# A four-layer graph network on one core: the first turning of x read from memory, row inverses on VectorE, the negated adjacency on ScalarE, and a new order of all parts

## What is computed

```python
# x (64,128,384), adj (64,128,128)
# L0: 12 heads: softmax over edges of (q k^T / sqrt(32) + beta*adj, masked where adj is 0), times v
# L1, two times: u = masked sums of (h Wl^T) h^T and (h Wr^T) h^T;  e = exp(u) * adj
#     attention = e / (sum(e) + 1e-10);  h = relu(layer_norm(attention @ h_lin))
# L2, two times (the digraph layer):
u = einsum('bid,bjd->bij', h, h) / temper
a = softmax(u, axis=-1)
delta = a * adjacency_matrix
attn = delta / (sum(delta, axis=-1) + 1e-10)
ctx = (attn*upper) @ hl + diag(attn) * hs + (attn*lower) @ hr
h = relu((ctx - mean) / sqrt(var + 1e-12) * g + beta)
# L3: 12 heads: softmax(q k^T * 384**-0.5 + adj) @ v, then @ Wo.T + bo
x = layernorm(x + L0(x, adj)); x = layernorm(x + L1(x, adj)); x = layernorm(x + L2(x, adj)); x = layernorm(x + L3(x, adj))
```

## Time and profile before

| what | value |
|---|---|
| median of 3 runs | 2648.01 us (2646.37 to 2648.55) |
| the profiled execution: its time | 2648.33 us |
| the profiled execution: its span, first to last instruction | 2646.3 us |
| PE busy | 2513.5 us, 95% |
| POOL, DVE, ACT busy | 2230.9, 2112.3, 2075.7 us |
| mean granted TensorE clock | 0.984 of 2.4 GHz |

### The profile page before, as it was taken

One profiled execution on the slowest core, in us unless ns is written; L12 is line 12 of the kernel. 1 busy time (PEld: TensorE's weight loads), 2 busy tenths in 40 slices (PEclk: granted clock), 3 DMA queues, 4 the chain that ended last, 5 costly groups with the idle time before them and its releaser, 6 DMA issues.

```text
span 2646.3 us, 91774 instructions
## 1 busy us (share of the span) xinstructions
PE 2513.5 (95%) x33856; PEld 1892.1 (71%) x33856; DVE 2112.3 (80%) x8230; ACT 2075.7 (78%) x5844; POOL 2230.9 (84%) x3340
## 2 busy tenths in 40 slices
PE   5799999999999999999999999999999999999985
PEld 4667677777777777777777777777777777777753
DVE  6687787877778888888888888888888888888874
ACT  6667877778778888888888788788788888888765
POOL 5488888888888898898888888888888888888874
PEclk9899999999999999999999999999999999999997
DMA  6834545545445555545545555554545555554533
GB/s 176 176 68 83 97 85 97 96 83 97 89 87 97 95 90 97 97 89 95 97 89 100 93 90 98 96 91 93 96 95 92 93 99 88 96 97 88 94 55 71
DMA packets 846822, 251.63 MB, mean 95 GB/s; under 512 B 805552, under 2 KB 845616, under 8 KB 846384
## 3 DMA queue, kind: packets, MB, share of 16 engines
q1 hardware_dynamic: 837920, 230.83, 50.3%
q10 hardware_dynamic: 8464, 14.94, 1.9%
HBM read 35.92 MB, written 12.58 MB: 18 GB/s over the span
## 4 chain that ended last, share of the span: by engine, by line
POOL 35%; PE 23%; DVE 16%; ACT 13%; issue 7%; DMA 5%; SPq 1%; DVEq 0%; ACTq 0%; POOLq 0%
POOL region L750 6%; ACT region L870 5%; DMA region<-region 4%; POOL region L739 4%; DVE region L1138 4%; PE bank L966 3%; PE bank L957 3%; PE bank L968 3%; PE bank L967 3%; PE bank L959 3%; PE bank L958 3%; ACT region L876 3%; POOL ab L766 3%; POOL region L790 2%; DVE small L1144 2%
## 5 line engine op out<-in xcount | busy, mean ns | idle before, releaser
L957 PE MATMUL bank<-region,w_hi 128*128 128x128 f16 x3960 | 690.4, 220 | 35.6 <-DVE w_lo L1075 14.0
L959 PE MATMUL bank<-region,w_lo 128*128 128x128 f16 x3960 | 690.0, 220 | 0.0
L958 PE MATMUL bank<-region,w_hi 128*128 128x128 f16 x3960 | 690.0, 220 | 0.0
L966 PE MATMUL bank<-w_hi,region 128*128 128x384 f16 x1815 | 595.5, 328 | 10.4 <-DMA region<-region 9.2
L967 PE MATMUL bank<-w_lo,region 128*128 128x384 f16 x1815 | 594.3, 327 | 0.0
L968 PE MATMUL bank<-w_hi,region 128*128 128x384 f16 x1815 | 594.2, 327 | 0.0
L750 POOL TENSOR_TENSOR region<-region 128x512 f16<-128x512 f32 x330 | 382.9, 1161 | 117.7 <-ACT region L876 116.6
L870 ACT ACTIVATE region<-region,small 128x128 f32<-128x128 f32 x1320 | 419.2, 389 | 53.6 <-DVE small L1144 44.1
L957 PEld LDWEIGHTS bank<-region,w_hi 128*128 128x128 f16 x3960 | 389.4, 98 | 60.8 <-issue 36.2
L958 PEld LDWEIGHTS bank<-region,w_hi 128*128 128x128 f16 x3960 | 389.8, 98 | 14.8 <-issue 9.9
L959 PEld LDWEIGHTS bank<-region,w_lo 128*128 128x128 f16 x3960 | 389.9, 98 | 0.0
(11 more groups left out here) (246 smaller groups left out, 8238.0 us busy)
## 6 DMA issues: line engine op xcount, KB each, us to landing
region<-region SPq DMA_TRANSPOSE x825, 3.0
last_unit<-w_dram ACTq DMA_DIRECT2D x19, 576.0 KB, 6.2
x<-x_dram SPq DMA_DIRECT2D x55, 192.0 KB, 2.3
out_dram<-region SPq DMA_DIRECT2D x55, 192.0 KB, 2.2
adj<-adj_dram SPq DMA_DIRECT2D x55, 64.0 KB, 2.2
mask<-adj_t_dram SPq DMA_DIRECT2D x55, 64.0 KB, 2.4
rows<-rows_dram ACTq DMA_DIRECT2D x5, 576.0 KB, 4.4
last_unit<-last_unit SPq DMA_TRANSPOSE x135, 3.1
```

Of the source, the lines that this page charges most:

```text
L957: pe.matmul(dst, lhsT=w_hi[:, w, k, cols], rhs=t_hi[u][:, k, :], start=(k == 0), stop=False)
L958: pe.matmul(dst, lhsT=w_hi[:, w, k, cols], rhs=t_lo[u][:, k, :], start=False, stop=False)
L959: last = pe.matmul(dst, lhsT=w_lo[:, w, k, cols], rhs=t_hi[u][:, k, :], start=False, stop=(k == DT - 1))
L966: pe.matmul(dst, lhsT=t_hi[u][:, k, :], rhs=w_hi[:, w, k, :], start=(k == 0), stop=False)
```

## The change

1. The host also passes x turned (`x_t_dram`). A new SP part `load_turned` loads it into the unit's `z` buffer, after norm 3 of unit i-7. ACT casts from there straight into the place that the transpose filled, and POOL writes the low half beside it. `turn` 0 on SP is gone, and projections 0 to 2 wait for POOL instead of a landing. The plain load of x and adj is a part of its own now, behind ACT's first cast; `bias_x` 0 on POOL and `masks` on DVE wait for it.
2. `denominator` is gone from POOL; its two steps follow on DVE behind the row sum, the inverse with `reciprocal`.
3. `minus_adjacency` goes from POOL to ACT.
4. The waits for weights go by the place of a weight in each engine's queue.
5. `PERIOD`, `SHIFTED` and nearly all wanted times in `PARTS` are new. Of the table two rows stand here for the rest.

```diff
-PERIOD = 22.1046
+PERIOD = 22.0572
-    (POOL, "sums", 0): (-457.777, 0.870, 0.950, ((VECTOR, "delta_di", 0),), ()),
+    (VECTOR, "delta_di", 0): (-124.527, 0.500, 0.580, ((SCALAR, "u_di", 0),), ()),
...
-            def load(i, k):
+            def load_turned(i, k):
                 if i == UNITS - 1:
                     sp.wait_ge(w_lo_made, NW)
                 if i >= UNITS:
-                    sp.wait_ge(*mixed_out.at(i - UNITS, "added", 3))
+                    sp.wait_ge(*scalar_done.at(i - UNITS, "normed", 3))
+                sp.dma_start(x_t[i % UNITS], x_t_d[i]).then_inc(loaded.of(i), 16)
+
+            def load(i, k):
+                sp.wait_ge(*cast.at(i, "x", 0))
                 sp.dma_start(x[i % UNITS], x_d[i]).then_inc(loaded.of(i), 16)
                 sp.dma_start(adj[i % UNITS], adj_d[i]).then_inc(loaded.of(i), 16)
...
+                if k == 0:
+                    pool.tensor_tensor(t_lo[u], x_t[u], t_hi[u], ALU.subtract).then_inc(low_made.of(i), 1)
+                    return
...
-                pool.tensor_scalar(minus_adj[u], adj[u], -1.0, None, ALU.mult).then_inc(gpsimd_done.of(i), 1)
-
-            def denominator(i, layer):
-                u = i % UNITS
-                pool.wait_ge(*mixed_out.at(i, "delta_di", layer))
-                pool.tensor_scalar(col(u, DENOM), col(u, ZSUM), 1e-10, col(u, DSUM), ALU.mult, ALU.add).then_inc(gpsimd_done.of(i), 1)
-                pool.wait_ge(*gpsimd_done.at(i, "sum", layer))
-                pool.tensor_tensor(col(u, INVERSE), col(u, DENOM), constant(MINUS_ONE), ALU.pow).then_inc(gpsimd_done.of(i), 1)
...
                 if k == 0:
-                    act.wait_ge(*loaded.at(i, "in"))
-                    src = x
+                    act.wait_ge(*loaded.at(i, "turned"))
+                    act.activation(t_hi[i % UNITS], x_t[i % UNITS], ACT.Copy).then_inc(cast.of(i), 1)
+                    return
...
+                act.activation(minus_adj[u], adj[u], ACT.Copy, scale=-1.0).then_inc(scalar_done.of(i), 1)
...
-                pe.wait_ge(*landed.at(i, "x", TURN_OF[w]))
+                if TURN_OF[w] == 0:
+                    pe.wait_ge(*low_made.at(i, "x", 0))
+                else:
+                    pe.wait_ge(*landed.at(i, "x", TURN_OF[w]))
...
+                dve.wait_ge(*numbers.at(i, "row sum", layer))
+                dve.tensor_scalar(col(u, DENOM), col(u, ZSUM), 1e-10, col(u, DSUM), ALU.mult, ALU.add).then_inc(numbers.of(i), 1)
+                dve.wait_ge(*numbers.at(i, "denominator", layer))
+                dve.reciprocal(col(u, INVERSE), col(u, DENOM)).then_inc(mixed_out.of(i), 1)
```

More of the change, by code:

```diff
@@ L134 @@
-    (VECTOR, "scores", 0): (-259.672, 0.850, 0.420, ((PE, "scores", 0), (VECTOR, "masks", 0)), ()),
-    (SYNC, "store", 0): (-259.643, 0.500, 2.300, ((SCALAR, "norm", 3),), ()),
-    (POOL, "bias_x", 0): (-258.884, 0.961, 1.245, ((POOL, "turn", 0),), ()),
-    (VECTOR, "add_bias", 14): (-251.016, 0.460, 0.560, ((PE, "project", 14), (POOL, "low", 12)), ()),
-    (SCALAR, "scores", 3): (-247.039, 1.860, 2.040, ((VECTOR, "scores", 3),), ()),
-    (VECTOR, "gain", 1): (-242.458, 0.916, 1.240, ((POOL, "inner", 1),), ()),
@@ new lines @@
+    (PE, "mix", 0): (-423.646, 0.680, 0.900, ((POOL, "bias", 5), (VECTOR, "delta_gcn", 0)), ()),
+    (POOL, "turn_delta", 1): (-399.969, 1.120, 1.360, ((SYNC, "delta", 1),), ()),
+    (VECTOR, "project", 2): (-394.972, 0.464, 0.742, ((SCALAR, "project", 2),), ()),
+    (SYNC, "scores", 1): (-384.079, 1.240, 4.000, ((POOL, "scores", 1), (PE, "attend", 0)), ()),
+    (SCALAR, "turn", 4): (-304.817, 0.412, 0.600, ((VECTOR, "gain", 2),), ()),
+    (POOL, "low", 12): (-301.610, 0.880, 1.120, ((SCALAR, "project", 12),), ()),
@@ new lines @@
+    (POOL, "scores", 2): (-113.386, 1.150, 1.420, ((SCALAR, "scores", 2),), ()),
+    (POOL, "low", 11): (-112.825, 0.880, 1.120, ((SCALAR, "project", 11),), ()),
+    (POOL, "bias_x", 0): (-112.365, 0.961, 1.245, ((SYNC, "load", 0),), ()),
+    (SCALAR, "project", 3): (-112.067, 0.387, 0.680, ((PE, "project", 3),), ()),
+    (POOL, "bias", 8): (-108.510, 0.955, 1.090, ((SCALAR, "project", 8),), ()),
+    (POOL, "bias", 10): (-107.287, 0.955, 1.090, ((SCALAR, "project", 10),), ()),
+    (SCALAR, "spread", 0): (-106.788, 0.830, 0.950, ((VECTOR, "residual", 0),), ()),
@@ new lines @@
+    (PE, "mix", 2): (-61.289, 0.975, 1.250, ((POOL, "turn_delta", 0), (POOL, "low", 9), (POOL, "low", 11)), ()),
+    (VECTOR, "gain", 0): (-55.345, 0.919, 1.243, ((POOL, "inner", 0),), ()),
+    (PE, "u_di", 1): (-54.142, 0.512, 0.720, ((SYNC, "turn", 4),), ()),
+    (SYNC, "delta", 1): (-53.701, 1.250, 3.000, ((VECTOR, "delta_low", 1),), ()),
+    (SCALAR, "spread", 1): (-51.267, 0.830, 0.950, ((VECTOR, "residual", 1),), ()),
+    (VECTOR, "project", 6): (-51.081, 0.466, 0.745, ((SCALAR, "project", 6),), ()),
@@ new lines @@
+    (PE, "project", 13): (-44.868, 1.466, 1.660, ((SYNC, "turn", 4),), ()),
+    (SCALAR, "turn", 3): (-43.965, 0.413, 0.600, ((SCALAR, "norm", 1),), ()),
+    (PE, "mix", 3): (-43.391, 0.975, 1.250, ((POOL, "turn_delta", 1), (POOL, "low", 12), (POOL, "low", 14)), ()),
+    (SYNC, "scores", 4): (-39.779, 1.240, 4.000, ((POOL, "scores", 4), (PE, "attend", 3)), ()),
+    (POOL, "scores", 3): (-38.186, 1.150, 1.420, ((SCALAR, "scores", 3),), ()),
+    (POOL, "residual", 2): (-34.059, 1.050, 1.150, ((SCALAR, "spread", 2),), ()),
@@ new lines @@
+    (PE, "project", 18): (7.331, 1.466, 1.660, ((SYNC, "turn", 6),), ()),
+    (POOL, "low", 9): (11.541, 0.880, 1.120, ((SCALAR, "project", 9),), ()),
+    (VECTOR, "scores", 2): (12.329, 0.850, 0.420, ((PE, "scores", 2), (POOL, "scores", 1)), ()),
+    (POOL, "residual", 1): (13.829, 1.050, 1.150, ((SCALAR, "spread", 1),), ()),
+    (SCALAR, "project", 13): (15.792, 0.387, 0.680, ((PE, "project", 13),), ()),
+    (VECTOR, "inner", 3): (17.429, 0.560, 0.720, ((PE, "mix", 3), (POOL, "bias", 13), (VECTOR, "delta_low", 1)), ()),
@@ new lines @@
+    (SCALAR, "project", 9): (21.661, 0.420, 0.530, ((VECTOR, "add_bias", 9),), ()),
+    (POOL, "low", 17): (23.023, 0.880, 1.130, ((SCALAR, "project", 17),), ()),
+    (SCALAR, "spread", 3): (49.145, 0.830, 0.950, ((VECTOR, "residual", 3),), ()),
+    (SYNC, "turn", 1): (51.159, 1.240, 3.600, ((POOL, "turn", 1),), ()),
+    (SCALAR, "attend", 5): (56.907, 0.165, 0.450, ((PE, "attend", 5),), ()),
+    (VECTOR, "project", 3): (63.996, 0.465, 0.743, ((SCALAR, "project", 3),), ()),
+    (VECTOR, "scores", 1): (67.729, 0.850, 0.420, ((PE, "scores", 1), (POOL, "scores", 0)), ()),
@@ L295 @@
+    (POOL, "low", 0): (856.688, 0.880, 1.130, ((SCALAR, "project", 0),), ()),
 }
@@ L663, in low_of, with nth @@
             return v_lo[u][:, :, 0:HD]
+        def nth(engine, w):
+            return 1 + [k for name, k, _ in sequence(engine) if name == "weight"].index(w)
         def load_weight(eng, n):
```

404 lines of the change are left out of this document (186 added, 218 removed), and 60 rows, old and new, of the table SHIFTED.

## The result

The changed kernel takes 2625.46 us (median of 4 runs, 2621.49 to 2626.07), the kernel before beside it 2647.19 (4 runs, 2642.60 to 2648.55). The ratio is 0.9915, its 95% interval 0.990 to 0.993: faster by 22 us. 2636 was forecast, in a range of 2616 to 2656. The direction and the range held; the forecast of -12 was about half of what came.

The account below looks back on a forecast made before the run. PE, 98.6% busy in the middle, was taken as the bound, leaving its idle and lower-clock time. Start -3, filling -2, end -2 and middle -5 summed to -12 us from 2648.0: 2636 us, range 2616 to 2656.

Parts of the forecast that it names:

- the term for the middle: 200 to 2500 us: order and shorter POOL queues change 44.4 us of PE idle time; -5 us, between -20 and +15.
- What bounds the kernel: PE is 98.6% busy from 800 to 2500 us; only its idle time and lower-clock time can be won.
- The start: Before 25 us: PE starts near 9.2 us instead of 14.03, V's projection first; -3 us.
- filling: While the pipeline fills, POOL's negation and denominator-inverse pairs leave the chain that ended last; -2 us, between 0 and -8.
- Less than 21 us of idle from 25 to 100: Sign for the filling: PE's idle time from 25 to 100 us, 23.7 us before, falls below 21.
- The turned load: Per unit, a transpose goes and a longer-waiting load comes; 0 us, between -2 and +1 per handover.
- POOL, DVE, ACT: POOL falls from 88% to 82% in the middle, DVE rises to about 85%, ACT gets 17 us; nothing in the middle.
- The end: Last 146 us: three denominator-inverse pairs leave POOL on the chain that ended last; -2 us, between -8 and +6.
- Greater gain: Rival: lighter SP and POOL queues remove half the middle's idle time and filling shortens 8 us; 2620 us, chance 0.12.
- Shorter distances: Rival: fewer projections between attend 5 and projection 18 make PE stand at projection 18; 2664 us, chance 0.16.
- The middle takes it back: Rival: one more small wait per unit cancels the 4 to 7 us from the ends; 2646 us, no change, chance 0.18.
- it doesn't do what it says: Rival: the turned load lands late at the start, PE starts no earlier than 14 us; 2639 us, no separate chance.

Follow-up runs that it names:

- old_order_pool: Kernel before, old order held, with denominator and inverse moved from POOL to DVE and the negation to ACT, x still turned by a transpose: 2651.28 us, ratio 1.0033.
- less_pool: Changed kernel without the add of L3's output bias on POOL, about 0.9 us a unit less: 2624.76 us, ratio 0.9913.
- not_turned: Changed kernel, its order held, with only the turned load undone (x loaded plain and turned by a transpose): 2798.07 us, ratio 1.0581.

## Where the prediction was right, and the step that failed

The step that failed is the term for the middle, the -5 us that stood for 200 to 2500 us and leaned on POOL's lighter queue. The runs show 14 to 19 us there, most of it from 200 to 800 us, and POOL's relief alone doesn't bring it. The other terms held in size, -7 in the sum and about 8 in the trace; that the time still fell into the range says nothing for the middle's term. By part:

**What bounds the kernel**: right. PE went from 98.6 to 98.9% in the middle, its work didn't change, and the gain is idle time and time at the lower clock, as the split of 22.2 and 4.8 us shows.

**The start**: right in its mechanism. PE, then DVE, in order of time:

```profile
8.80 0.48 PE L971 MATMUL bank<-w_hi,region 128*128 128x384 f16 x1 [8.80 <-DVE w_lo L1083]
```

```profile
13.86 1.36 DVE L1083 SCALAR_TENSOR_TENSOR w_lo<-last_unit,w_hi 128x1152 f16<-128x1152 f32 x1 [0.90 <-ACT w_hi L825]
```

8.80 us was measured where 9.2 was forecast, V's projection first, and seven projections stand ahead of the first scores, as counted. But V's took 2.83 us, since its steps start 0.32 us apart, where they are 0.163 apart later; the steps of 128 columns behind it stay slow too, 0.11 apart until 13.4 us and 0.056 after. Before, the slow piece ran from 14.03 to 18.3. The profile's granted clock reads 1.00 in both pieces, but the spacing is that of the lower of the two levels, 1.2 GHz. So the kernel still pays for some 4.5 us of it at the start, only earlier. I had put K's low half at its old time, 12.42 us; it is 1.4 later, since ACT now has V's projection to cast ahead of K's weight. The first mask took 0.30 and 0.91 us, 1.2 in all and 0.6 more than with POOL idle, where the forecast had 1.2 us of delay. The first scores start at 21.6 us instead of 21.88: the lead is projections in hand, not scores. Of the 7.2 us, 4.0 are gone by 50 us and 4.6 by 100, and from 50 to 75 us PE is as idle as ever. 25 to 50 and 50 to 75 us, after and then before:

```profile
25.00:50.00 25.00, 19.12 (x313) 15.83 (x310) 18.81 (x73) 17.26 (x44) 19.34 (x19) 0.93 0.46 101
50.00:75.00 25.00, 6.47 (x169) 4.44 (x170) 13.04 (x72) 19.26 (x54) 14.31 (x21) 0.52 0.93 199
```

```profile
25.00:50.00 25.00, 23.16 (x403) 19.58 (x401) 15.29 (x64) 16.66 (x41) 19.56 (x19) 1.00 0.52 105
50.00:75.00 25.00, 6.67 (x153) 4.25 (x151) 11.44 (x66) 20.19 (x54) 15.08 (x18) 0.62 0.79 181
```

Start and filling together gave -4.0 us of idle time up to 200 us, or 49 matmuls (2052 instead of 2003), 3.6 us; -5 was forecast for the two. "Less than 21 us of idle from 25 to 100" was wrong (28.3), because the two terms were not independent: what the start brings, the filling partly takes.

**The turned load**: right with its zero, by PE's single wait of 0.6 us for it and SP's of 4.3. Two of its prices were low: it takes 0.58 us of SP's queue in the median instead of 0.33, and lands in 2.9 us instead of 2.3. Its bounds hold only inside its order: between -2 and +1 us per handover is far from the 4.9 us per unit at which SP stood in the old one.

**POOL, DVE, ACT**: right in size. POOL fell to 82.5% in the middle (82 forecast), DVE rose to 85%, and the new steps by line, busy us and mean ns of one, are:

```profile
L1202 DVE TENSOR_SCALAR small<-small 128x1 f32<-128x1 f32 x110 | 23.6, 214 | 3.9
L1204 DVE RECIPROCAL small<-small 128x1 f32<-128x1 f32 x110 | 18.0, 163 | 3.7
L897 ACT ACTIVATE mask<-adj 128x128 f32<-128x128 f32 x55 | 17.0, 309 | 0.2 <-DVE region L1187 0.2
```

The inverse was taken from the right row; the denominator is 0.05 us longer, 128 x 0.377 = 48 us instead of 42. The copy was 0.309 us where an exponential's 0.267 stood for it. Neither touches the sum. **The end** gave 4.1 us of idle time where 2 was forecast.

**The middle**: here the forecast failed, by size. "Nothing but order and shorter queues on POOL can change it" was right, and so was the bound of -20; the term of -5 lay just below the middle of its range of -20 to +15, with the words "POOL's lighter queue speaks for the lower half". Measured are 14.7 us from 200 to 800 and 4.5 after, -19 in this trace, and about -14 by the medians, if the 5 us by which the traces differ more than the medians are all put here (22 less 4 and 4). The mis-sized term lies in the passage, and the reason given for the term was the wrong one: POOL's relief alone is +8 us (old_order_pool), and -0.9 us of POOL in the new kernel gives nothing (less_pool). I spread the middle's 44 us of idle time evenly over its repeats and didn't read that 21.4 us of it lay in 600 us before 800, 3.6 per 100 us as against 1.35 later. Nor did I read the clock of 0.99 in that stretch as time to be won: it is 1.00 now, and 4.9 of the 14.7 us are that.

**The rivals.** *Greater gain* had the mechanism right in part (from 200 to 2400 us the idle time falls by a third, 43.4 before and 29.0 after by the table above, where the rival asked for half) and named POOL's and SP's queues as its cause, which the runs refute for POOL. *Shorter distances* didn't happen in the order as it came: from 800 to 2400 us projections wait 1.8 us for landings in all, in 5 waits. A wait of its kind comes once the turned load is taken away (not_turned, 1.8 us in 32 units), but at projection 0 and not at projection 18, where the rival put it. *The middle takes it back* and *it doesn't do what it says* are refuted by the middle's idle time and by the matmul at 8.80.

The sum of terms as such is to be mistrusted too. Measured on the old order, the reordering of the start, which brings PE forward by only 0.3 us there, is no gain (+5 us, within 0.2%), POOL's relief is +8, and the whole of the new code +317; and with its own order the same code is 22 us faster.

## What to carry to other kernels

Where in-order queues are filled to 98% by a searched order, a change of code is hard to price apart from its new order: read the terms of the diff as conditions for a new order, and take their value from where the old order still idles, stretch by stretch, with the granted clock beside it. A queue next to the bound may be at 82% and yet have no room: in a fixed order half a microsecond more per unit was nearly hidden, and 2.3 were not. To judge such a part, add and remove work there that nobody waits for; a single part moved without its order shows only what the mismatch costs. And to credit a change of code with a gain that came together with a new search, search for the old code once more as well, which no run here does.

## What the hardware showed beside this

DVE's second step of a mask took 0.35 us with POOL idle and 0.90 while POOL made low halves; in the changed kernel the first mask falls in POOL's work. DVE, and POOL, in order of time:

```profile
16.12 0.91 DVE L1119 SCALAR_TENSOR_TENSOR mask<-adj,minus_beta,mask 128x128 f32<-128x128 f32 x1
```

```profile
14.32 4.36 POOL L746 TENSOR_TENSOR region<-z,region 128x384 f16<-128x384 f32 x4 [0.55 <-ACT region L841]
```

By the Trainium skill (SBUF — State Buffer, section Who interferes with whom) GpSimd and a DVE instruction with two SBUF inputs exclude each other on a shared read interface; both traces agree with it for this step. The mask's first step, with one SBUF input, slowed down as much, from 0.23 to 0.94 us, in the kernel before.

Both loads of 192 KB take more of SP's queue than the one before did, 0.58 us in the median for the turned x and 0.57 for the plain one instead of 0.33, and the turned x landed in 2.9 us, in the median, where the plain x of the same 192 KB took 2.5 in the same trace and 2.3 before. The transposes left over landed in 3.1 instead of 3.0. No run here tells whether that is the neighbours in the new order or the source.

```profile
region<-region SPq DMA_TRANSPOSE x770, 3.1
...
z<-x_t_dram SPq DMA_DIRECT2D x55, 192.0 KB, 2.9
x<-x_dram SPq DMA_DIRECT2D x55, 192.0 KB, 2.5
```

On DVE a step on 128x1 with a column as its second operand took 0.214 us and the reciprocal beside it 0.163, both on the same 128x1.
